# Segment sums of a four-layer graph network: gathered rows divided into three bf16 parts, one product of 390 columns a tile

## Chip, cores and metric

The kernel runs on one core of a Trainium2 chip, in one launch. The metric is the device time of a run in microseconds. Before the change three runs without a profile took 9422.37, 9434.25 and 9440.75 us; the median is 9434.25 us. The profile shown here is one further execution under the profiler.

## What is computed

6250 nodes with 128 features, and 106250 edges (`src`, `dst`) sorted by `dst`. Each of four layers is a function of `relu(layernorm(x))` that is added to `x`. What matters here are the sums over edges that each layer contains, cut to their core:

```python
support = segment_sum(xt[src], dst)                          # L0 (also the sum of edge weights a node, for L3)
out     = segment_sum(xw[src] * alpha[:, :, None], dst)      # L1, attention, alpha = softmax over a node's edges
aggA    = segment_sum(x[src] * mask_t, dst)                  # L2, for four edge types t
aggB    = segment_sum(x[dst] * mask_t, src)                  # L2, the other direction
out     = segment_sum(h[src] * norm[:, None], dst)           # L3, twice; norm = dinv[src] * w * dinv[dst]
```

`segment_sum(a, d)` adds row e of `a` to node `d[e]`. L2's weights are multiplied into the table of rows first, so that its two sums gather from a table with one row for each node and type.

## The kernel before

**Tiles and walks.** Edges lie in 832 tiles of 128, one edge a partition. A sum over the edges is a *walk*: 208 chunks of CT = 4 tiles, in a loop of 52 rounds whose body holds RING = 4 chunks (u = 0 to 3). The walks with a gather are l0, g1 (attention scores), l2, l2b (the other direction, over a list sorted by `src` that the kernel makes itself), l3a and l3b, in this order; gb, the attention sum, reads rows that were stored. Nodes lie in 49 blocks of 128. Because the edges are sorted, the 512 edges of a chunk fall into one block or into two; the second one is the `more` loop, which 48 chunks of a walk enter.

**A chunk, by engine.** Each engine has its program written by hand, and they meet at semaphores.
GpSimd (`gather`, L543; the DMA at L550) issues four indirect DMAs a chunk, each of 128 rows of 128 fp32 into GATHERED, a ring of four chunks. It waits for `free`, which says that the chunk four earlier has left its slot, and for `idx`.
ScalarE (`indices`, L834) writes the row numbers of the chunk four ahead (L831) when a chunk has landed. In l0 `weights_beside` (L859) also copies the edge weights beside the rows, as column 128.
VectorE (`aggregate` in the vector program) compares the destinations with the numbers of a block: `onehots` makes the 512-column one-hot matrix OH of the *next* chunk, in one operation (L1198) or, in l3a and l3b, in four that multiply by the edge weight as well (L1204). Then it waits for the products of this chunk and adds them to the node rows (L1220), which lie in ACC, X or T.
TensorE (`sums`, L653; the product at L658) multiplies the four one-hots with the four tiles of rows, fp32, 128 columns (129 in l0), added up in one PSUM bank; two banks take turns.
The number of further blocks, their number before this chunk and the first block come from a table, RANGES, which each engine reads into registers (L303, L306).

The order on VectorE in a chunk:

```python
onehots(c + 1, block_values((u + 1) % sets)[2], 1 - p, weights, column).then_inc(wk.onehot, 1)
hold(dve, wk.sums, c + 1)
add(first, p).then_inc(wk.added, 1)
with others(u % sets):            # the second block, where there is one
    onehots(c, b, p, weights, column).then_inc(wk.more_onehot, 1)
    hold(dve, wk.more_sums, before + w + 1)
    add(b, p).then_inc(wk.more_added, 1)
dve.nop(nofuse=True).then_inc(wk.free, 1)
```

**Work beside l0.** In l0's loop VectorE also prepares the list for l2b: in the first half, every second chunk, a comparison of 832 keys (L1356) and a count (L1365); in the second half a comparison, a scan (L1403), a product and a sum (L1406, L1408).

## Time and profile before

| | us |
|---|---|
| median of three runs without profile | 9434.25 (9422.37 to 9440.75) |
| span of the profiled execution | 11044.3 |
| time of the profiled execution outside its span | not recorded |
| GpSimd busy | 5820.6 (53%) |
| TensorE busy, products | 4003.0 (36%) |
| VectorE busy | 3958.5 (36%) |
| ScalarE busy | 1410.5 (13%) |
| TensorE clock granted, mean | 0.568 of full speed |

The profiled execution took longer than the runs. The stretches of the walks in its span, by the first and last gather: l0 from 268 to 1540 us, g1 1691 to 3223, gb some 3250 to 4280, the writes of the list 4283 to 5534, l2 to 6822, l2b 6829 to 8123, l3a 8220 to 9530, l3b 9657 to 10955. Between 4280 and 5000 the spike loop and the typed tables run.

A row of the trace gives an engine, a line of the kernel and the tiles by name (PS is PSUM, OH the one-hots, EX, H and T scratch). Idle time stands with what ended it: "issue" means that nothing visible did, "DVEq" a step of VectorE's own sequencer, "remote" a source that the trace does not know. A product of fp32 shows as two records, so a chunk's four are x8.

### The profile page before, as it was taken

What the parts mean: (1) busy time and instruction counts of PE and PEld (TensorE: products, weight loads), DVE (VectorE), ACT (ScalarE), POOL (GpSimd) and SP (SyncE); (2) the same over time, 40 slices, a digit from 0 to 9 for tenths busy, and PEclk for the clock granted to TensorE, in tenths of its full rate; (3) what the DMA queues carried; (4) which work ended last, traced back from release to release, by engine and by line L of the source; (5) the groups of instructions that cost most, each with busy time, mean ns of one, the idle gap of its engine ahead of it and who ended that gap; (6) DMA issues with size and microseconds to landing.
All of it is one profiled execution on the core that took longest, in us unless ns stands there. A gap on an engine that the chain in (4) does not pass through costs nothing. (4 is left out here: it accounts for less than half of the span.)

```text
span 11044.3 us, 116200 instructions
## 1 busy us (share of the span) xinstructions
PE 4003.0 (36%) x18072; PEld 3408.2 (31%) x18073; DVE 3958.5 (36%) x9685; ACT 1410.5 (13%) x3057; POOL 5820.6 (53%) x5941
## 2 busy tenths in 40 slices
PE   1333423333345554321033443333333333333332
PEld 1333323333335552010033333333323333233332
DVE  5335664444445557920011111111122222422224
ACT  1000011111124445710000000000000000000000
POOL 0667744555430003777766666666645565356664
PEclk6555556666665555555556665555555555555555
DMA  1111103333332221000011111111111111111111
GB/s 42 43 42 42 44 25 92 93 90 91 89 88 81 81 81 36 1 21 21 7 54 52 53 53 47 42 42 43 43 39 40 41 42 42 35 41 42 42 43 41
DMA packets 364720, 548.58 MB, mean 50 GB/s; under 512 B 124102, under 2 KB 217114, under 8 KB 364650
## 3 DMA queue, kind: packets, MB, share of 16 engines
q0 software_dynamic: 186368, 330.08, 11.1%
q1 hardware_dynamic: 148330, 190.56, 5.6%
q10 hardware_dynamic: 29952, 27.28, 1.0%
q14 instruction: 60, 0.49, 0.0%
q8 instruction: 10, 0.16, 0.0%
HBM read 448.36 MB, written 99.13 MB: 50 GB/s over the span
## 5 line engine op out<-in xcount | busy, mean ns | idle before, releaser
L658 PE MATMUL PS<-GATHERED,OH 128*128 128x128 f32 (+1 forms) x10240 | 2403.2, 416 | 4359.3 <-issue 1547.1
L658 PEld LDWEIGHTS PS<-GATHERED,OH 128*128 128x128 f32 x10240 | 2145.9, 312 | 4664.6 <-issue 2130.2
L550 POOL DMA_INDIRECT GATHERED<-row_tab,IDX x2496 | 2464.6, 987 | 1899.6 <-issue 1030.8
L550 POOL DMA_INDIRECT GATHERED<-gat_tab,IDX x832 | 784.8, 943 | 898.4 <-DVEq L1505 509.8
L575 POOL DMA_INDIRECT list_dram<-REC_NOW,PLACE_NOW x832 | 912.5, 1097 | 313.8 <-issue 258.4
L550 POOL DMA_INDIRECT GATHERED<-typed_b_tab,IDX x832 | 817.9, 983 | 483.1 <-issue 241.0
L550 POOL DMA_INDIRECT GATHERED<-typed_tab,IDX x832 | 808.9, 972 | 479.6 <-issue 234.8
L715 PE MATMUL PS<-IDENT,GATHERED 128*128 128x128 f32 x3328 | 588.1, 355 | 968.6 <-DVEq L1505 823.1
L1220 DVE TENSOR_TENSOR X<-X,PS 128x128 f32 x512 | 146.6, 286 | 2013.7 <-remote 1305.8
L715 PEld LDWEIGHTS PS<-IDENT,GATHERED 128*128 128x128 f32 x3328 | 544.3, 188 | 1012.4 <-issue 1010.5
L1204 DVE TENSOR_SCALAR OH<-IOTA,DSTF,WF 128x128 f32 x2048 | 601.1, 361 | 678.5 <-issue 648.1
L658 PE MATMUL PS<-T,OH 128*128 128x132 f32 x2048 | 541.6, 446 | 343.5 <-DVE OH L1198 292.0
L1220 DVE TENSOR_TENSOR T<-T,PS 128x128 f32 x512 | 145.7, 285 | 1237.2 <-remote 688.6
L658 PEld LDWEIGHTS PS<-T,OH 128*128 128x128 f32 x2048 | 466.0, 330 | 376.7 <-DVE OH L1198 336.4
L569 POOL COPY PLACE_NOW<-PLACE 128x16 int32 (+1 forms) x52 | 12.1, 232 | 1059.0 <-DVE ACC L1220 1059.0
L831 ACT ACTIVATE IDX<-SRCF 128x4 int32 x816 | 167.5, 205 | 2648.9 <-DMA GATHERED<-row_tab,IDX 2500.9
L1478 DVE CUSTOM_DVE_ANT_0 H<-PS,EQ 128x512 f32<-128x512 f32 x520 | 328.1, 687 | 404.8 <-remote 296.0
L1478 DVE CUSTOM_DVE_ANT_0 H<-PS,SCR 128x512 f32<-128x512 f32 x504 | 318.1, 687 | 402.9 <-remote 339.7
L1198 DVE TENSOR_TENSOR OH<-IOTA,DSTF 128x512 f32 (+1 forms) x512 | 352.5, 688 | 90.0 <-issue 86.2
L1220 DVE TENSOR_TENSOR ACC<-ACC,PS 128x129 f32 (+1 forms) x512 | 146.9, 287 | 662.9 <-PE PS L658 294.1
L754 PE MATMUL PS<-ACC,WSB 128*128 128x448 bf16 x350 | 157.8, 555 | 283.3 <-ACT ACC L975 282.0
L1198 DVE TENSOR_TENSOR OH<-IOTA,REC 128x512 f32 (+1 forms) x256 | 177.4, 693 | 172.9 <-issue 171.3
(243 smaller groups left out, 3912.5 us busy)
## 6 DMA issues: line engine op xcount, KB each, us to landing
gat_rows<-GATHERED SPq DMA_DIRECT2D x208, 264.0 KB
GATHERED<-gat_rows SPq DMA_DIRECT2D x208, 264.0 KB, 2.8
GATHERED<-row_tab,IDX POOLq DMA_INDIRECT x2496
ROWI<-dst_rows ACTq DMA_DIRECT2D x208, 128.0 KB
ROWI<-dst_rows SPq DMA_DIRECT2D x208, 128.0 KB
GATHERED<-gat_tab,IDX POOLq DMA_INDIRECT x832
list_dram<-REC_NOW,PLACE_NOW POOLq DMA_INDIRECT x832
GATHERED<-typed_tab,IDX POOLq DMA_INDIRECT x832
```

The source lines that it names most:

```text
L550: pool.indirect_dma_start(out=rows, out_offset=None, in_=table, in_offset=bass.IndirectOffsetOnAxis(ap=IDX[:, k:k + 1], axis=0),).then_inc ...
L569: pool.tensor_copy(PLACE_NOW[:, now:now + BATCH], PLACE[:, bass.ds((2 * i + k) * BATCH, BATCH)]).then_inc(batch_copied, 1)
L575: pool.indirect_dma_start(out=list_dram, out_offset=bass.IndirectOffsetOnAxis(ap=PLACE_NOW[:, now + t:now + t + 1], axis=0), in_=REC_NOW[: ...
L658: last = mm(bank(p)[:, 0:r.shape[1]], onehot(p, t), r, start=(t == 0), stop=(t == CT - 1))
L715: last = nc.tensor.transpose(bank(HEADS * (u % 2) + h)[:, t * P:(t + 1) * P], col.to_broadcast([P, P]), IDENT[:, :])
L754: last = mm(SPIKES[:, k, :], IDB, SPK[t % 2][:, k * (GB * D // 2):(k + 1) * (GB * D // 2)], start=(t == 0), stop=(t == LIF_T - 1))
L831: nc.scalar.activation(IDX[:, u * CT:(u + 1) * CT], column[:, bass.ds((RING * (i + 1) + u) * CT, CT)], ACT.Copy).then_inc(wk.idx, 1)
L1198: return v.tensor_tensor(onehot(p, 0, CT).rearrange("p (t w) -> p t w", t=CT), IOTA[:, bass.ds(b * P, P)].rearrange("p (o w) -> p o w", o= ...
L1204: last = v.tensor_scalar(onehot(p, t), IOTA[:, bass.ds(b * P, P)], DSTF[:, bass.ds(c * CT + t, 1)], weights[:, bass.ds(c * CT + t, 1)], AL ...
L1220: return v.tensor_tensor(dest, dest, bank(p)[:, 0:F], ALU.add)
L1478: last = v.tensor_tensor_reduce(out=unused[h], in0=bank(HEADS * (u % 2) + h), in1=(EQ if u % 2 == 0 else SCR)[:, :], scale=1.0, scalar=-BI ...
```

## The change

Each gathered row is divided into three bf16 parts whose sum is the row: hi = bf16(row), rest = row - hi, mid = bf16(rest), low = rest - mid. The parts stand side by side in PARTS, 130 columns apart (SEC), so that one bf16 product of 3 x 130 = 390 columns replaces the fp32 product; VectorE first adds the three sections of the bank (a reduction to COMBINED) and then adds that to the node rows. It applies to l0, l2, l2b, l3a and l3b. The attention walk gb keeps its fp32 form (`exact`).

Of a chunk, ScalarE makes hi and mid, VectorE rest (in place in GATHERED) and low. The one-hots become bf16 and are no longer weighted: in l3a and l3b VectorE multiplies the gathered rows by the edge weights instead, before the division. In l0 the weights are divided once, ahead of the walk, and ScalarE copies their three parts into column 128 of each section. PARTS holds two chunks; `parts_free` says that VectorE has finished the chunk two earlier, `free` (the ring slot) now comes with low. The table of ranges holds 16-bit numbers in rows of eight.

VectorE's order in a chunk (`chunks`):

```diff
+            if not exact:
+                if weights is not None:
+                    weigh_rows(i + (1 if u == RING - 1 else 0), c + 1, (u + 1) % RING)
+                rest(c + 1, (u + 1) % RING)
-            onehots(c + 1, block_values((u + 1) % sets)[2], 1 - p, weights, column).then_inc(wk.onehot, 1)
+            onehots(c + 1, block_values((u + 1) % sets)[2], 1 - p, column, exact).then_inc(wk.onehot, 1)
+            if not exact:
+                low(c + 1, (u + 1) % RING)
...
-            add(first, p).then_inc(wk.added, 1)
+            combine(first, p, (part_combined, c + (wk.splits * NCH + 1)), wk.added)
...
-            dve.nop(nofuse=True).then_inc(wk.free, 1)
+            dve.nop(nofuse=True).then_inc(parts_free, 1)
```

Its new functions:

```diff
+                def combine(b, p, made, added):
+                    v.tensor_reduce(COMBINED[:, 0:F], bank(p)[:, 0:NP3 * SEC].rearrange("p (k f) -> p f k", k=NP3)[:, 0:F, :],
+                                    axis=AX.X, op=ALU.add).then_inc(made[0], 1)
+                    hold(dve, *made)
+                    dest = result(b)
+                    v.tensor_tensor(dest, dest, COMBINED[:, 0:F], ALU.add).then_inc(added, 1)
+
+                def weigh_rows(i, c, u):
+                    hold(dve, wk.gathered[u], 16 * CT * (i + (wk.rounds * NIT + 1)))
+                    v.tensor_tensor(rows_of(u), rows_of(u), per_edge(weights, c, D), ALU.mult).then_inc(row_weighed, 1)
+
+                def rest(c, u):
+                    hold(dve, part_hi, c + (wk.splits * NCH + 1))
+                    v.tensor_tensor(rows_of(u), rows_of(u), parts_of(u)[:, 0, :, :], ALU.subtract).then_inc(part_rest, 1)
+
+                def low(c, u):
+                    hold(dve, part_mid, c + (wk.splits * NCH + 1))
+                    v.tensor_tensor(parts_of(u)[:, 2, :, :], rows_of(u), parts_of(u)[:, 1, :, :],
+                                    ALU.subtract).then_inc(wk.free, 1)
```

ScalarE's work for a chunk (`indices`):

```diff
+                def chunk(i, u, last_):
+                    c = RING * i + u
+                    hold(act, wk.gathered[u], 16 * CT * (i + (wk.rounds * NIT + 1)))
+                    if not last_:
+                        next_indices(wk, column, i, u)
+                    hold(act, parts_free, c + (wk.splits * NCH + 1))
+                    if weighed:
+                        hold(act, row_weighed, c + ((wk.rounds - 1) * NCH + 1))
+                    nc.scalar.activation(parts_of(u)[:, 0, :, :], rows_of(u), ACT.Copy).then_inc(part_hi, 1)
+                    if weights:
+                        nc.scalar.activation(parts_of(u, D + 1)[:, :, :, D],
+                                             WP[:, bass.ds(c * (CT * NP3), CT * NP3)].rearrange("p (t k) -> p k t", k=NP3),
+                                             ACT.Copy).then_inc(weight_kept, 1)
+                    hold(act, part_rest, c + (wk.splits * NCH + 1))
+                    nc.scalar.activation(parts_of(u)[:, 1, :, :], rows_of(u), ACT.Copy).then_inc(part_mid, 1)
```

The operand of TensorE's product, and what VectorE does ahead of l0:

```diff
+            def part_rows(u, t):
+                at = ((u % 2) * CT + t) * NP3 * SEC
+                return [PARTS[:, at:at + NP3 * SEC]]
...
+            dve.wait_ge(s_stored, 16)
+            split(WF[:, :], WREST, [WP.rearrange("p (t k) -> p k t", k=NP3)[:, k, :] for k in range(NP3)])
             dve.sem_inc(counted, 1)
+            step(v.memset(PARTS[:, :], 0.0))
+            dve.sem_inc(w_split, 1)
+            dve.sem_inc(parts_free, 2)
```

The first place is VectorE's program in the loop of l3b, from the read of the table to the add of a chunk, before (L1204 the weighted one-hots, L1220 the add; ISA rows are register steps):

```order
L303 TENSOR_LOAD RANGES
L306 ISA
L1204 TENSOR_SCALAR OH<-IOTA,DSTF,WF 128x128
L1204 ISA
L1204 TENSOR_SCALAR OH<-IOTA,DSTF,WF 128x128
L1204 ISA
L1204 TENSOR_SCALAR OH<-IOTA,DSTF,WF 128x128
L1204 ISA
L1204 TENSOR_SCALAR OH<-IOTA,DSTF,WF 128x128
L306 ISA
L54 REGISTER_ALU [waits sums_l3b]
L1220 ISA [waits added_l3b]
L1220 TENSOR_TENSOR T<-T,PS 128x128
```

and with the change, from the wait for the gather to the add (L1240 the weighing, L1244 rest, L1212 the one-hot, L1248 low, L1232 the reduction, L1236 the add):

```order
L1240 ISA [waits gathered_l0_2]
L1240 TENSOR_TENSOR GATHERED<-GATHERED,WF 128x4x128
L32 REGISTER_ALU
L1244 TENSOR_TENSOR GATHERED<-GATHERED,PARTS 128x4x128 [waits part_hi]
L298 ISA
L1212 TENSOR_TENSOR OH<-IOTA,DSTF 128x512
L1248 TENSOR_TENSOR PARTS<-GATHERED,PARTS 128x4x128 [waits part_mid]
L298 ISA
L32 REGISTER_ALU [waits sums_l0]
L1232 TENSOR_REDUCE COMBINED<-PS 128x128 [waits added_l3b]
L1236 ISA [waits part_combined]
L1236 TENSOR_TENSOR T<-T,COMBINED 128x128
```

Between the table and the wait for the products stood four one-hots and no wait; now four operations and three waits stand there, two of them for ScalarE, and the add itself has become two operations with a wait between them.

The second place is ScalarE's program in the loop of l3b, the first chunks before (L831 the row numbers):

```order
L831 ISA [waits gathered_l0_0]
L831 ACTIVATE IDX<-SRCF 128x4
L831 ISA [waits gathered_l0_1]
L831 ACTIVATE IDX<-SRCF 128x4
```

and one chunk with the change (L852 hi, L858 mid):

```order
L837 ISA [waits gathered_l0_0]
L837 ACTIVATE IDX<-SRCF 128x4
L32 ISA
L32 REGISTER_ALU [waits part_free]
L852 ACTIVATE PARTS<-GATHERED 128x4x128 [waits row_weighed]
L858 ACTIVATE PARTS<-GATHERED 128x4x128 [waits part_rest]
```

Behind the row numbers of one chunk the next chunk's wait for its gather came at once; now two copies with three waits for VectorE come between.

## Rows read from the trace of the kernel before

**Rows 1.** The page of the profiled execution: its span and part 1.

```profile
span 11044.3 us, 116200 instructions
...
PE 4003.0 (36%) x18072; PEld 3408.2 (31%) x18073; DVE 3958.5 (36%) x9685; ACT 1410.5 (13%) x3057; POOL 5820.6 (53%) x5941
```

**Rows 2.** Groups of instructions: gathers and list writes; name xcount | busy, mean ns | idle, releasers.

```profile
L550 POOL DMA_INDIRECT GATHERED<-row_tab,IDX x2496 | 2464.6, 987 | 1899.6 <-issue 1030.8 <-DVEq L1242 621.8 <-DMA row_tab<-T 224.3
...
L575 POOL DMA_INDIRECT list_dram<-REC_NOW,PLACE_NOW x832 | 912.5, 1097 | 313.8 <-issue 258.4 <-POOL REC_NOW L571 28.7 <-remote 26.7
L550 POOL DMA_INDIRECT GATHERED<-typed_b_tab,IDX x832 | 817.9, 983 | 483.1 <-issue 241.0 <-DVEq L1242 229.9 <-ACT IDX L827 6.9
L550 POOL DMA_INDIRECT GATHERED<-typed_tab,IDX x832 | 808.9, 972 | 479.6 <-issue 234.8 <-ACT IDX L831 126.6 <-DVEq L1242 118.1
L550 POOL DMA_INDIRECT GATHERED<-gat_tab,IDX x832 | 784.8, 943 | 898.4 <-DVEq L1505 509.8 <-issue 237.1 <-DMA gat_tab<-ACC 150.9
```

**Rows 3.** Timeline in l3a: start us, us, engine, line, operation [idle before <-releaser].

```profile
9012.65 1.11 DVE L1204 TENSOR_SCALAR OH<-IOTA,DSTF,WF 128x128 f32 x4 [0.67 <-issue]
...
9013.82 2.08 PE L658 MATMUL PS<-GATHERED,OH 128*128 128x128 f32 x8 [4.09 <-DVE OH L1204]
...
9020.98 0.29 DVE L1220 TENSOR_TENSOR T<-T,PS 128x128 f32 x1 [7.21 <-remote]
...
9022.03 0.94 POOL L550 DMA_INDIRECT GATHERED<-row_tab,IDX  x1 [3.96 <-DVEq L1242]
```

**Rows 4.** Gathers in l0's first half, in its second, and in l3a.

```profile
L550 POOL DMA_INDIRECT GATHERED<-row_tab,IDX x403 | 397.1, 985 | 228.2 <-issue 125.6 <-DVEq L1242 97.7 <-ACT IDX L831 2.5
...
L550 POOL DMA_INDIRECT GATHERED<-row_tab,IDX x414 | 477.0, 1152 | 150.0 <-issue 123.4 <-DVEq L1242 25.6 <-ACT IDX L831 0.9
...
L550 POOL DMA_INDIRECT GATHERED<-row_tab,IDX x824 | 780.2, 947 | 520.0 <-DVEq L1242 259.6 <-issue 250.4 <-ACT IDX L831 7.4
```

**Rows 5.** Timeline in l2b: gathers, one-hots and an add.

```profile
7301.71 0.94 POOL L550 DMA_INDIRECT GATHERED<-typed_b_tab,IDX  x1 [0.31 <-issue]
7301.77 0.69 DVE L1198 TENSOR_TENSOR OH<-IOTA,REC 128x512 f32 x1
...
7302.52 2.08 PE L658 MATMUL PS<-GATHERED,OH 128*128 128x128 f32 x8 [8.71 <-DVE OH L1198]
...
7304.79 0.29 DVE L1220 TENSOR_TENSOR X<-X,PS 128x128 f32 x1 [2.33 <-issue]
7305.78 0.69 DVE L1198 TENSOR_TENSOR OH<-IOTA,REC 128x512 f32 x1 [0.70 <-issue]
7305.83 1.46 POOL L550 DMA_INDIRECT GATHERED<-typed_b_tab,IDX  x1 [0.68 <-issue]
```

**Rows 6.** Groups of instructions, shapes apart: prices of VectorE's and ScalarE's operations.

```profile
L1198 DVE TENSOR_TENSOR OH<-IOTA,DSTF 128x512 f32 x504 | 347.0, 688 | 86.5 <-issue 83.3 <-DVE H L1365 1.5
...
L831 ACT ACTIVATE IDX<-SRCF 128x4 int32 x816 | 167.5, 205 | 2648.9 <-DMA GATHERED<-row_tab,IDX 2500.9 <-issue 138.5 <-DMA GATHERED<-gat_tab,IDX 5.7
...
L1220 DVE TENSOR_TENSOR X<-X,PS 128x128 f32 x512 | 146.6, 286 | 2013.7 <-remote 1305.8 <-PE PS L658 607.1 <-issue 98.2
...
L1403 DVE TENSOR_TENSOR_SCAN EX<-ONE,H,EX 128x832 f32<-128x832 f32 x50 | 97.5, 1951 | 9.8 <-issue 5.7 <-DVE EX L1356 4.1
...
L1356 DVE TENSOR_SCALAR EX<-EX,KCOL 128x832 f32<-128x832 f32 x102 | 73.0, 716 | 32.6 <-issue 32.6
L1534 DVE TENSOR_REDUCE AT_EDGE<-PS 128x32 f32<-128x96 f32 x256 | 65.9, 258 | 206.1 <-PE PS L723 90.3 <-issue 87.4 <-DVE AT_EDGE L1534 28.4
...
L1365 DVE TENSOR_REDUCE H<-EX 128x832 f32 x52 | 53.0, 1020 | 11.8 <-DVE EX L1356 6.8 <-issue 5.0
...
L811 ACT ACTIVATE GATHERED<-H 128x896 f32 x24 | 22.6, 941 | 0.0
```

**Rows 7.** Busy time and clock in l3a; then the bf16 product of the spike counts.

```profile
8225.00:9525.00 1300.00, 489.35 (x2016) 434.00 (x2016) 363.69 (x1257) 41.87 (x204) 780.17 (x824) 0.53 0.14 42
...
L754 PE MATMUL PS<-ACC,WSB 128*128 128x448 bf16 x350 | 157.8, 555 | 283.3 <-ACT ACC L975 282.0 <-issue 1.2
```

More of the change, by code:

```diff
@@ L31 @@
 I16 = mybir.dt.int16
+U16 = mybir.dt.uint16
 BF16 = mybir.dt.bfloat16
@@ L545, in gather @@
                 hold(pool, wk.free, c + 1)
-                hold(pool, wk.idx, c + 1)
+                hold(pool, wk.idx, c + (wk.splits * NCH + 1))
                 for t in tiles:
@@ L656, in sums @@
                 for t in range(CT):
-                    r = rows(t)
-                    last = mm(bank(p)[:, 0:r.shape[1]], onehot(p, t), r, start=(t == 0), stop=(t == CT - 1))
+                    for n, r in enumerate(rows(t)):
+                        last = mm(bank(p)[:, 0:r.shape[1]], onehot(p, t, 1, r.dtype == F32), r, start=(t == 0 and n == 0),
+                                  stop=(t == CT - 1 and n == len(rows(t)) - 1))
                 return last
@@ L671, in chunk @@
                     hold(pe, wk.added, c + 1)
-                    sums(lambda t: rows(u, t), wk.onehot, c, u % 2).then_inc(wk.sums, 1)
+                    sums(lambda t: rows(u, t), wk.onehot, c + wk.splits * NCH, u % 2).then_inc(wk.sums, 1)
                     with others(u % sets):
@@ L845, in indices @@
                     start += n
+                for u in range(RING):
+                    chunk(NIT - 1, u, True)
             for req in requests["before_l0"]:
@@ L851, in _ @@
                 answer(*req)
-            wk = walks["l0"]
-            first_indices(wk, SRCF)
-            def weights_beside(i, last_):
-                for u in range(RING):
-                    c = RING * i + u
-                    hold(act, wk.gathered[u], 16 * CT * (i + 1))
-                    nc.scalar.activation(G3[:, u * CT:(u + 1) * CT, D], WF[:, bass.ds(c * CT, CT)],
-                                         ACT.Copy).then_inc(weight_kept, 1)
-                    if not last_:
-                        next_indices(wk, SRCF, i, u)
-            with act.Fori(0, NIT - 1) as i:
-                weights_beside(i, False)
-            weights_beside(NIT - 1, True)
+            act.wait_ge(w_split, 1)
+            indices("l0", weights=True)
             for req in requests["l0_sums"]:
@@ L1024, in _ @@
             dense(dn, denses["l3a"], 4)
-            indices("l3a")
+            indices("l3a", weighed=True)
             for req in requests["l3a"]:
@@ L1028, in _ @@
             dense(dn, denses["l3b"], 5)
-            indices("l3b")
+            indices("l3b", weighed=True)
             for req in requests["l3b"]:
@@ L1216, in aggregate @@
                 wk = walks[name]
+                exact = ahead is not None
                 def add(b, p):
@@ L1249, in aggregate @@
                     read(0, 0, table)
-                onehots(0, block_values(0)[2], 0, weights, column).then_inc(wk.onehot, 1)
+                if not exact:
+                    if weights is not None:
+                        weigh_rows(0, 0, 0)
+                    rest(0, 0)
+                onehots(0, block_values(0)[2], 0, column, exact).then_inc(wk.onehot, 1)
+                if not exact:
+                    low(0, 0)
                 start = 0
```

110 lines of the change are left out of this document (66 added, 44 removed).

## The prediction

> **What bounds the kernel now.** I read the page first. GpSimd is the busiest engine, 5820.6 us of a span of 11044.3 us; TensorE, which the change relieves, is busy for 36% of it [rows 1]. Nearly all of GpSimd's time is row gathers, 832 in each of six walks over the edges, and 832 writes of a list [rows 2]. A walk has 208 chunks of 4 gathers.
>
> Next the timeline of an l3a stretch. While nothing is late, gathers take 0.94 us with 0.30 us between (as in [rows 5]), 1.25 us each and 5.0 us a chunk; TensorE's four products of a chunk take 2.08 us. Then the pattern breaks: TensorE is done at 9015.90, VectorE adds those sums only at 9020.98, released by nothing that the trace knows, and GpSimd waits 3.96 us for the ring slot that VectorE frees behind the add [rows 3]. I take these stalls for the recording's own: the median run without a profile is 9434.25 us, 1610 us shorter than the recorded span (the record gives no other time for that execution). GpSimd's idle time before gathers and list writes sums to 4074.5 us; less 5824 x 0.305 us of usual gap (1776) and two waits for a table's store (224.3 + 150.9, [rows 2]), 1923 us are left. If all that the median saves is of these waits, 313 us of them remain in it, 0.25 us a chunk.
>
> The changed walks are therefore bound by **GpSimd's issue**: 4 x (mean gather + 0.305) is 5.11 us a chunk in l2 and 5.15 in l2b [rows 2], 5.16 in l0's first half, 5.83 in its second and 5.01 in l3a and l3b [rows 4]. I work out differences in these numbers and add them to the median; added to the recorded span they would carry the recorder's stalls along.
>
> **Why gathers differ in length.** A gather that starts 0.05 us behind the start of a one-hot, which has two SBUF inputs, takes 1.46 us instead of 0.94; a one-hot that starts 0.06 us behind a gather keeps its 0.69 us, and the gather its 0.94 [rows 5]. l0's second half, where scans of 1.95 us run on VectorE [rows 6], has a mean of 1.152 us [rows 4]. So a two-input VectorE operation on SBUF delays a gather that starts while it runs. One-hots run 256 times a walk, 208 for first blocks and 48 for second ones (512 adds for two walks [rows 6]), 1.23 a chunk. In l2b they cost 4 x (0.983 - 0.944) = 0.16 us a chunk, 0.13 us for each.
>
> **The change, per chunk.**
> Removed: the four fp32 products (2.08 us) become four bf16 ones of 390 columns. By columns that is 4 x 390 against four passes of 4 x 128, so 2.08 x 1560/2048 = 1.6 us at the same clock (0.53 granted, close to the 1.2 GHz level [rows 7]). Bounds: 2.2 us by the bf16 product of 448 columns, 0.555 us each [rows 7], and 0.8 at twice the clock. For first blocks this lies under VectorE's next chunk and is worth nothing; only a second block waits for it.
> Added on ScalarE: two copies of 512 elements. 896 take 0.941 us and 4 take 0.205, so by the line between them 0.62 [rows 6]; ends 0.55 and 0.72.
> Added on VectorE: rest and low, 512 elements and two inputs each, 0.69 us as the one-hot [rows 6]. In l3a and l3b also the weighing, 0.69, while four one-hots of together 1.11 [rows 3] become one of 0.69. The add of 0.29 becomes a reduction of 384 PSUM elements and an add of 0.29. The reduction lies between 96 elements at 0.258 and 832 at 1.020, by that line 0.56 [rows 6]; ends 0.45 and 0.75, should the stride between the three sections help or hurt.
> Moved: a ring slot is freed behind low instead of behind the add. That helps GpSimd only where slots were short, the 0.25 us above at most. The 16-bit range table is read in as many loads as before; I cost it at nothing, as it lies between VectorE's commands in the start below.
>
> Now the order on VectorE. While it splits chunk c+1 it waits twice for ScalarE, whose first copy may begin only when VectorE has finished chunk c-1, and in l3 only behind the weighing. All that is queued behind these waits, the add of chunk c among it, stands still. For a change of engine I allow 0.15 us, between one-hot to product, 0.06 [rows 3], and product to add, 0.19 (7302.52 + 2.08 to 7304.79 [rows 5]), with ends 0.06 and 0.30; within VectorE 0.10.
> l3: start 0.70 (0.67 seen [rows 3]) + weigh 0.69 + (0.15 + copy 0.62 + 0.15) + rest 0.69 + (0.15 + second copy 0.62 + 0.15, over the one-hot's 0.69) + low 0.69 + reduce 0.56 + 0.10 + add 0.29 = 5.56. Second blocks, 48 in 208: 0.69 + 1.6 + 0.24 + 0.56 + 0.10 + 0.29 = 3.48, or 0.80 a chunk. Together **6.4 us**, over GpSimd's 5.0, so the chain of VectorE and ScalarE sets the pace.
> l2, l2b: no weighing, and the first copy (0.92 and 0.10 of waits) runs beside the start: 1.02 + 0.69 + 0.92 + 0.69 + 0.95 + 0.80 = 5.1. GpSimd meets two more two-input operations and the short add: 5.13 + 2.2 x 0.13 = **5.42**, the larger of the two.
> l0: 5.1 plus the bucket work beside, (0.72 + 1.02)/2 + 0.1 = 1.0 in the first half and (0.72 + 1.95 + 1.02 + 1.02)/2 + 0.1 = 2.5 in the second (its product and sum taken as the count of as many elements, 1.02 [rows 6]), less 0.2 for the copy that runs beside it: **5.9** and **7.4**.
>
> Sum: l3a and l3b 416 x (6.4 - 5.01) = 578; l2 and l2b 416 x (5.42 - 5.13) = 121; l0 104 x (5.9 - 5.16) + 104 x (7.4 - 5.83) = 240; splitting the weights and clearing the parts ahead of l0, five operations of 1 to 2 us, 10. That is +949, and 9434 + 949 = **10380 us**.
> Ends: with handovers of 0.06, a reduction of 0.45 and a start of 0.5, l3 takes 5.65 and l0 5.3 and 6.8: 266 + 121 + 15 + 101 + 10 = +513, less the waits that the median may still have in walks that VectorE now paces (0.25 x 624 = 156), +357. With handovers of 0.30, copies of 0.72, a reduction of 0.75 and second blocks 0.4 longer: l3 7.5, l2 6.1, l0 7.0 and 8.5, +1920. Each end needs all at once; half of the way to them is 10090 and 10870, this case's own range.
>
> A rule weighed here. One-hots take 0.69 us in the mean of 504 [rows 6], though gathers fill three quarters of the time and one is seen to start inside a gather without loss [rows 5]. The Trainium skill (SBUF — State Buffer, "Who interferes with whom") says that a VectorE instruction with two SBUF inputs contends with a GpSimd instruction that reads SBUF, and that whichever starts second fully blocks until the first has ended. The late gather agrees with it; the other direction, VectorE held by a running gather, no row here shows.
>
> **Rivals.**
> A. *GpSimd still paces every walk* (0.14). VectorE's commands overlap more than I allow and l3 stays near 5.5 us. Against it: each step of the chain waits for one on another engine. Then l3 costs 416 x (5.55 - 5.01) = 225, l2 121, l0 130, and 10 ahead: 9920.
> B. *Blocked both ways* (0.03). A two-input operation that starts inside a gather waits for its rest. Gathers fill 0.944 of 1.25 us, so each waits 0.76 x 0.47 = 0.36 us: 1.5 us for 4.2 operations in l3, 1.2 for 3.2 elsewhere, of which l2's slack takes 0.3. That is 416 x 1.5 + 416 x 0.9 + 208 x 1.2 = 1250 more, 11630. The one-hots at 0.69 speak against. It is also what the page's rule gives if it holds in both directions.
> C. *Handovers dearer* (0.09). Registers and waits cost 0.3 us each, six to eight a chunk: l3 7.2, l2 5.9, l0 6.7 and 8.2, so 911 + 320 + 407 + 10: 11080.
> D. *Faster* (0.04). The 313 us that the median can hold are real waits for ring slots in VectorE's order. Freed behind low, not behind products and add, the five changed walks lose them: 0.25 x 1040 = 260, 9170. It decides only where VectorE's chain stays under 5.0 us a chunk; l0's second half, with 2.5 us of bucket work on top, speaks against it, and so does every sum above.
> E. *No difference* (0.03). The chain fits under the gathers, and the ring waits saved pay for the longer gathers: 9434.
>
> **How the numbers follow.** The likeliest case has 0.67 and gives the time. The range 9870 to 11000 holds nearly all of it, A's middle and the cheaper part of C; B, D, E and the rest, about 0.2, are out. A measurement can tell about 0.2% (19 us) from no change: faster 0.04 (D), within it 0.03 (E), slower 0.93.
>
> **What would show it.** In the changed profile, away from the recorder's stalls: gathers of l3a and l3b that wait for VectorE's low; an l3 chunk of 6.4 us; l0's second half the slowest stretch; l2's gathers at a mean near 1.05 us; copies at 0.62, the reduction at 0.56 and a chunk's four products at 1.6 us; VectorE busy some 2000 us more, TensorE less. The prediction is wrong if VectorE stands idle in l3 while gathers follow each other at 1.25 us, or if rest, the one-hot or low take much less than 0.69 us.

## The result and the profile after

| | before | changed |
|---|---|---|
| median of four runs each, us | 9435.38 | 10835.39 |
| lowest to highest, us | 9422.37 to 9440.75 | 10834.68 to 10839.15 |
| ratio, with its interval | | 1.1486 (1.147 to 1.1502) |
| span of the profiled execution, us | 11044.3 | 10834.0 |

The change makes the kernel slower by 1400 us. The forecast was 10380 us in a range of 9870 to 11000: the direction and the range hold, but a loss of 946 us was forecast, some 450 less than came.

The page of the changed kernel: span, part 1, two rows of part 4 (the chain that ended last), and the groups that answer to [rows 2] and [rows 6].

```profile
span 10834.0 us, 121338 instructions
...
PE 3498.6 (32%) x12952; PEld 1802.1 (17%) x12953; DVE 6027.9 (56%) x11930; ACT 2636.4 (24%) x5137; POOL 6072.7 (56%) x5941
...
DVE 29%; issue 23%; DVEq 14%; POOL 13%; ACT 9%; PE 8%; DMA 2%; ACTq 0%; SPq 0%; POOLq 0%
DVEq L295 9%; POOL list_dram L576 8%; DVE COMBINED L1232 6%; DVE GATHERED L1244 6%; PE PS L659 6%; ACT PARTS L858 5%; POOL GATHERED L551 4%; ACT PARTS L852 3%; DVE GATHERED L1240 3%; DVE OH L1212 2%; DVE H L1533 2%; DVEq L34 2%; DVE PARTS L1248 1%; PE PS L721 1%; DMA GATHERED<-gat_tab,IDX 1%
...
L551 POOL DMA_INDIRECT GATHERED<-row_tab,IDX x2496 | 2562.0, 1026 | 2187.8 <-DVE PARTS L1248 1053.6
L659 PE MATMUL PS<-PARTS,OH 128*128 128x390 bf16 x5120 | 1880.5, 522 | 5451.6 <-issue 1578.3
L1244 DVE TENSOR_TENSOR GATHERED<-GATHERED,PARTS 128x512 f32<-128x512 f32 x1040 | 720.2, 693 | 1849.9 <-ACT PARTS L852 1703.1
...
L551 POOL DMA_INDIRECT GATHERED<-typed_tab,IDX x832 | 896.6, 1078 | 274.3 <-issue 233.7
L551 POOL DMA_INDIRECT GATHERED<-typed_b_tab,IDX x832 | 885.0, 1064 | 271.5 <-issue 228.6
...
L1232 DVE TENSOR_REDUCE COMBINED<-PS 128x128 f32<-128x384 f32 (+1 forms) x1280 | 708.7, 554 | 421.4 <-PE PS L659 417.2
```

Read them in this order. TensorE has 500 us less to do and VectorE 2070 us more [rows 1]. The row gathers, which in [rows 2] waited for VectorE only where its steps came late, now wait 1053.6 us for low (L1248), the operation that frees a ring slot; in l2 and l2b nearly all of their idle time is the usual 0.3 us gap, but each gather is longer (1.078 and 1.064 us, 0.972 and 0.983 before). Rest (L1244) waited 1703.1 us for ScalarE's first copy. In the chain that ended last VectorE's own queue (DVEq, its register and semaphore instructions) stands with 14%, of which the page puts 9% on L295; that line is the load of the range table.

A chunk of l3a in the timeline of the changed kernel (start us, us, engine, line, operation, [idle before <-releaser]; TensorE's weight loads left out):

```profile
8732.48 0.29 DVE L1236 TENSOR_TENSOR T<-T,COMBINED 128x128 f32 x1 [0.20 <-DVE COMBINED L1232]
...
8733.51 1.48 PE L659 MATMUL PS<-PARTS,OH 128*128 128x390 bf16 x4 [4.61 <-DVE T L1236]
...
8734.05 0.69 DVE L1240 TENSOR_TENSOR GATHERED<-GATHERED,WF 128x512 f32<-128x512 f32 x1 [1.28 <-issue]
8734.83 0.63 ACT L852 ACTIVATE PARTS<-GATHERED 128x512 bf16<-128x512 f32 x1 [3.84 <-DVE GATHERED L1240]
...
8735.57 0.69 DVE L1244 TENSOR_TENSOR GATHERED<-GATHERED,PARTS 128x512 f32<-128x512 f32 x1 [0.83 <-ACT PARTS L852]
8736.18 0.69 DVE L1212 TENSOR_TENSOR OH<-IOTA,DSTF 128x512 bf16 x1
8736.35 0.63 ACT L858 ACTIVATE PARTS<-GATHERED 128x512 bf16<-128x512 f32 x1 [0.89 <-DVE GATHERED L1244]
8736.43 1.25 POOL L551 DMA_INDIRECT GATHERED<-row_tab,IDX  x1 [0.30 <-issue]
...
8737.08 0.69 DVE L1248 TENSOR_TENSOR PARTS<-GATHERED,PARTS 128x512 bf16<-128x512 f32 x1 [0.22 <-ACT PARTS L858]
8737.69 0.55 DVE L1232 TENSOR_REDUCE COMBINED<-PS 128x128 f32<-128x384 f32 x1
8738.44 0.29 DVE L1236 TENSOR_TENSOR T<-T,COMBINED 128x128 f32 x1 [0.20 <-DVE COMBINED L1232]
8738.65 0.94 POOL L551 DMA_INDIRECT GATHERED<-row_tab,IDX  x1 [0.97 <-DVE PARTS L1248]
...
8740.09 0.69 DVE L1240 TENSOR_TENSOR GATHERED<-GATHERED,WF 128x512 f32<-128x512 f32 x1 [1.36 <-issue]
```

From one weighing to the next it is 6.04 us, and every step of the forecast's chain can be read: weigh, 0.09, copy 0.63, 0.11, rest, one-hot, 0.09 behind rest the second copy, 0.10, low, reduction, 0.20, add. TensorE's 1.48 us lie beside it. Then comes the long one: 1.28 and 1.36 us from the add to the next weighing, in which VectorE issues only register and semaphore work.

### The profile page after: what moved, and what is told of

It reads as the page before. It is cut to its first block, busy times and chain, and to the rows that moved or that the text cites. A ratio compares the mean times of both kernels' runs of the same rounds, so it can differ in the third digit from the quotient of the medians.

```text
span 10834.0 us, 121338 instructions
## 1 busy us (share of the span) xinstructions
PE 3498.6 (32%) x12952; PEld 1802.1 (17%) x12953; DVE 6027.9 (56%) x11930; ACT 2636.4 (24%) x5137; POOL 6072.7 (56%) x5941
## 4 chain that ended last, share of the span: by engine, by line
DVE 29%; issue 23%; DVEq 14%; POOL 13%; ACT 9%; PE 8%; DMA 2%; ACTq 0%; SPq 0%; POOLq 0%
DVEq L295 9%; POOL list_dram L576 8%; DVE COMBINED L1232 6%; DVE GATHERED L1244 6%; PE PS L659 6%; ACT PARTS L858 5%; POOL GATHERED L551 4%; ACT PARTS L852 3%; DVE GATHERED L1240 3%; DVE OH L1212 2%; DVE H L1533 2%; DVEq L34 2%; DVE PARTS L1248 1%; PE PS L721 1%; DMA GATHERED<-gat_tab,IDX 1%
## 5 line engine op out<-in xcount | busy, mean ns | idle before, releaser
L551 POOL DMA_INDIRECT GATHERED<-row_tab,IDX x2496 | 2562.0, 1026 | 2187.8 <-DVE PARTS L1248 1053.6
L659 PE MATMUL PS<-PARTS,OH 128*128 128x390 bf16 x5120 | 1880.5, 522 | 5451.6 <-issue 1578.3
L1244 DVE TENSOR_TENSOR GATHERED<-GATHERED,PARTS 128x512 f32<-128x512 f32 x1040 | 720.2, 693 | 1849.9 <-ACT PARTS L852 1703.1
L659 PEld LDWEIGHTS PS<-PARTS,OH 128*128 128x128 bf16 x5120 | 555.4, 130 | 6802.0 <-issue 5639.0
L852 ACT ACTIVATE PARTS<-GATHERED 128x512 bf16<-128x512 f32 x1040 | 656.0, 631 | 2872.8 <-DVE GATHERED L1240 1916.4
L551 POOL DMA_INDIRECT GATHERED<-typed_tab,IDX x832 | 896.6, 1078 | 274.3 <-issue 233.7
L858 ACT ACTIVATE PARTS<-GATHERED 128x512 bf16<-128x512 f32 x1040 | 655.2, 630 | 1499.3 <-DVE GATHERED L1244 1499.3
L1232 DVE TENSOR_REDUCE COMBINED<-PS 128x128 f32<-128x384 f32 (+1 forms) x1280 | 708.7, 554 | 421.4 <-PE PS L659 417.2
L1248 DVE TENSOR_TENSOR PARTS<-GATHERED,PARTS 128x512 bf16<-128x512 f32 x1040 | 720.0, 692 | 237.8 <-ACT PARTS L858 236.4
L1212 DVE TENSOR_TENSOR OH<-IOTA,DSTF 128x512 bf16 (+3 forms) x1024 | 703.3, 687 | 7.5
L1240 DVE TENSOR_TENSOR GATHERED<-GATHERED,WF 128x512 f32<-128x512 f32 x416 | 288.4, 693 | 631.8 <-issue 587.1
```

The lines of the kernel that those rows point to most:

```text
L551: pool.indirect_dma_start(out=rows, out_offset=None, in_=table, in_offset=bass.IndirectOffsetOnAxis(ap=IDX[:, k:k + 1], axis=0),).then_inc ...
L659: last = mm(bank(p)[:, 0:r.shape[1]], onehot(p, t, 1, r.dtype == F32), r, start=(t == 0 and n == 0), stop=(t == CT - 1 and n == len(rows(t ...
L852: nc.scalar.activation(parts_of(u)[:, 0, :, :], rows_of(u), ACT.Copy).then_inc(part_hi, 1)
L858: nc.scalar.activation(parts_of(u)[:, 1, :, :], rows_of(u), ACT.Copy).then_inc(part_mid, 1)
L1212: return v.tensor_tensor(onehot(p, 0, CT, exact).rearrange("p (t w) -> p t w", t=CT), IOTA[:, bass.ds(b * P, P)].rearrange("p (o w) -> p o ...
L1232: v.tensor_reduce(COMBINED[:, 0:F], bank(p)[:, 0:NP3 * SEC].rearrange("p (k f) -> p f k", k=NP3)[:, 0:F, :], axis=AX.X, op=ALU.add).then_i ...
```

## The experiments

Twelve runs in three lots; three of them repeat a kernel. The kernel before is run beside each lot, and gave 9434 us beside the first, 11005 beside the second and 10903 beside the third, each on another chip. So times are compared within a lot only. Each chip stood in one lot, so what belongs to the chip and what to other circumstances of a lot can't be told apart; "chip" below means both. In the code cuts `...` marks lines left out.

### First lot: which part of the change costs what

**e1_before_u16**: the kernel before with the range tables of the change (16 bits, 8 elements a chunk, of which 4 are read), and nothing else.

```diff
-        RANGES = sb("RANGES", [1, REGS * NCH], I32)
+        RANGES = sb("RANGES", [1, ROW * NCH], U16)
...
-                eng.load(regs[p], table[0:1, bass.ds(c * REGS, REGS)])
+                eng.load(regs[p], table[0:1, bass.ds(c * ROW, REGS)])
```

> The kernel before with nothing changed but the table of ranges: 16-bit numbers in rows of eight, as the change has it. Theory 1 (a read of the 16-bit table takes 0.95 us instead of 0.34 and that is a part of the change's loss): the gathered walks stay as they are, since GpSimd's 5.0 us a chunk covers VectorE's 2.5 to 3.1; gb, which has no gather and reads the table on three engines, loses about 1 us a chunk: 9640 us. Theory 2 (the reads are hidden; the prediction's chain of VectorE and ScalarE is merely longer): 9435 us.

Measured: 9547.53 us, ratio 1.0121 (1.0104 to 1.0138), so the table costs the old kernel 114 us. The trace's records of the loads to registers say why: on VectorE one takes 0.948 us in the median of 1464 (0.344 us for the 32-bit table in the profile of before), on ScalarE 0.887 (0.308), on TensorE 0.987 (0.332). The cost is smaller than the 9640 us expected, because the edge walk gb, the only one in which a load was expected to show, loses some 0.55 us a chunk and not 1: from the last gather of g1 to the first write of the list it takes 1085 us in e2 with the 32-bit table and 1199 in the changed kernel.

This profile has a second use. Its span is 9548.9 us, as long as its runs without a profile, and it has none of the stalls of [rows 3]. So it is the clean picture of the old order of work, but for the wider loads. The gathers of its l3b:

```profile
L551 POOL DMA_INDIRECT GATHERED<-row_tab,IDX x832 | 789.0, 948 | 380.3 <-issue 246.2 <-DMA row_tab<-T 127.1 <-DVEq L1243 7.0
```

They wait 7.0 us in all for the slot that VectorE frees behind products and add; in the other walks that the change touches it is 6.7 (l3a), 12.5 (l2), 15.2 (l2b) and 5.5 and 27.3 us (l0's halves). That is 74 us, and, apart from the ends of walks, about the most that any cheaper product could have given back while the gathers stay as they are.

The windows of e1, for l0 (two halves), g1, the edge walk gb, l2, l2b, l3a and l3b (columns: window, its length, busy time and count of PE, PEld, DVE, ACT and POOL, granted clock, DMA share, GB/s):

```profile
267.00:802.00 535.00, 258.32 (x1008) 224.62 (x1008) 211.02 (x354) 33.08 (x206) 408.53 (x416) 0.52 0.19 51
802.00:1412.00 610.00, 261.57 (x1020) 228.04 (x1020) 373.11 (x496) 33.05 (x205) 476.66 (x416) 0.51 0.17 45
1567.00:2607.00 1040.00, 588.26 (x3312) 530.74 (x3312) 685.65 (x2285) 221.04 (x458) 784.77 (x832) 0.75 0.52 134
2608.00:3801.00 1193.00, 605.11 (x3088) 516.03 (x3088) 575.57 (x1883) 415.94 (x722) 0.34 (x2) 0.50 0.26 70
5029.00:6083.00 1054.00, 562.68 (x2186) 448.91 (x2187) 246.58 (x508) 96.15 (x351) 800.74 (x832) 0.59 0.23 65
6092.00:7151.00 1059.00, 511.69 (x2040) 445.88 (x2040) 246.99 (x511) 41.91 (x204) 805.27 (x832) 0.54 0.20 51
7246.00:8290.00 1044.00, 514.16 (x2040) 451.86 (x2040) 355.77 (x1278) 41.87 (x204) 790.64 (x832) 0.51 0.20 52
8417.00:9459.00 1042.00, 514.19 (x2040) 450.79 (x2040) 355.06 (x1278) 41.87 (x204) 788.75 (x832) 0.52 0.20 52
```

And the same stages of the changed kernel:

```profile
274.00:880.00 606.00, 179.89 (x492) 53.82 (x492) 399.97 (x671) 152.81 (x405) 428.67 (x416) 0.50 0.17 45
880.00:1671.00 791.00, 188.28 (x516) 56.95 (x516) 575.34 (x824) 155.81 (x414) 448.67 (x416) 0.50 0.13 35
1847.00:2887.00 1040.00, 589.35 (x3312) 532.58 (x3312) 685.04 (x2286) 219.32 (x458) 784.94 (x832) 0.75 0.52 134
2888.00:4086.00 1198.00, 605.43 (x3088) 516.11 (x3088) 575.58 (x1881) 415.39 (x721) 0.34 (x2) 0.50 0.26 70
5313.00:6483.00 1170.00, 462.22 (x1155) 149.65 (x1155) 638.65 (x1167) 325.41 (x762) 895.96 (x832) 0.54 0.21 58
6502.00:7640.00 1138.00, 374.27 (x1013) 109.70 (x1014) 644.76 (x1174) 296.89 (x618) 884.67 (x832) 0.50 0.18 48
7738.00:9159.00 1421.00, 371.26 (x1004) 108.76 (x1004) 775.53 (x1366) 280.54 (x614) 837.05 (x832) 0.50 0.15 38
9305.00:10726.00 1421.00, 371.28 (x1004) 108.75 (x1004) 775.63 (x1367) 278.51 (x614) 845.74 (x832) 0.50 0.15 38
```

Divided by 208 chunks (104 for a half), before stood at 5.15 and 5.87 us in l0, 5.07 in l2, 5.09 in l2b and 5.01 in l3a and l3b; the changed kernel at 5.83 and 7.61, 5.63, 5.47 and 6.83. The stages differ by 252 us in l0, 195 in l2 and l2b together and 756 in l3a and l3b. With the 114 us of the table in the edge walk (the windows of 1193 and 1198 us both hold it) these make 1317 of the 1400 us; the rest lies outside these stretches, at starts and ends of walks, and was not taken apart.

**e2_after_i32**: the changed kernel with the 32-bit table of before; the loaded values go through a register of their own and a maximum with zero.

```diff
...
-                eng.load(regs[p], table[0:1, bass.ds(c * ROW, REGS)])
+                eng.load(raw[p], table[0:1, bass.ds(c * REGS, REGS)])
+                for loaded_, r in zip(raw[p], regs[p]):
+                    eng.reg_alu(r, loaded_, 0, ALU.max)
```

> The changed kernel with the table in 32-bit numbers as before, loaded into registers of their own and held at 0 or more by one register step each. Theory 1: l3a and l3b lose 0.6 us a chunk (6.83 to 6.2, 250 us together), l0 0.3 (60), l2 and l2b little (30), gb about 1 us (200): 10300 us. Theory 2: 10835 us, the chunk times unchanged.

Measured: 10397.72 us (10391.57 to 10401.34), ratio 1.1022 (1.1004 to 1.1041): 438 us below the changed kernel, where some 535 were expected. The width of a table of 208 rows is nearly a third of the whole loss. The timeline of e2 shows the step, and l3b's window the pace:

```profile
8822.33 0.29 DVE L1239 TENSOR_TENSOR T<-T,COMBINED 128x128 f32 x1 [0.20 <-DVE COMBINED L1235]
...
8823.38 0.69 DVE L1243 TENSOR_TENSOR GATHERED<-GATHERED,WF 128x512 f32<-128x512 f32 x1 [0.76 <-issue]
```

```profile
8978.00:10294.00 1316.00, 371.33 (x1004) 108.85 (x1004) 777.14 (x1369) 278.54 (x614) 909.10 (x832) 0.50 0.16 41
```

The start is 0.76 us where it was 1.28 to 1.36, and a chunk 1316/208 = 6.33 us instead of 6.83. In the trace's records the load takes 0.947 us of that start of 1.36 and 0.343 of the 0.76; the rest is 0.41 and 0.42, so the maximum with zero costs next to nothing here. Of the 438 us, 2 x 105 lie in l3a and l3b; in l0 the two halves go to 5.47 and 7.19 us, 80 us; the edge walk gives back 113.

**e3_after_i32_three**: e2 with the three parts multiplied one behind the other into the same 130 columns of the bank, 12 products a chunk instead of 4, so that TensorE adds the three sums and VectorE's reduction goes.

```diff
-                return [PARTS[:, at:at + NP3 * SEC]]
+                return [PARTS[:, at + k * SEC:at + (k + 1) * SEC] for k in range(NP3)]
...
-                    v.tensor_reduce(COMBINED[:, 0:F], bank(p)[:, 0:NP3 * SEC].rearrange("p (k f) -> p f k", k=NP3)[:, 0:F, :], axis=AX.X, op=ALU.add).then_inc(made[0], 1)
-                    hold(dve, *made)
-                    v.tensor_tensor(dest, dest, COMBINED[:, 0:F], ALU.add).then_inc(added, 1)
+                    add(b, p).then_inc(added, 1)
```

> As e2, and each tile's one product of 390 columns becomes three of 130 that add up in the same 130 columns of the bank; VectorE adds them to the node rows directly, without the reduction. If the chain on VectorE sets the pace, the reduction and the wait behind it (0.56 + 0.10, 1.23 times a chunk) come off l3a, l3b and l0: 0.8 x 624 = 500 us less than e2, about 9800; l2 and l2b stay at GpSimd's 5.4 us. If TensorE's products are on the path, 12 weight loads a chunk instead of 4 cost more than they give: the same as e2 or slower.

Measured: 9959.78 us, ratio 1.0558 (1.0541 to 1.0576), again 438 us less, where 500 were expected: 296 in l3a and l3b, 98 in l0, nothing in l2 and l2b. In its timeline TensorE's twelve products of 130 columns take 1.48 us together, as the four did: the 390 columns were no gain over three times 130.

**e4_after_i32_noweigh**: e2 without the weighing in l3a and l3b; the edge weights are left out of these two walks.

```diff
-            indices("l3a", weighed=True)
+            indices("l3a")
...
-                aggregate(name, lambda b: T[:, bass.ds(b * D, D)], D, WF)
+                aggregate(name, lambda b: T[:, bass.ds(b * D, D)], D)
```

> As e2, with the weighing of the gathered rows left out of l3a and l3b (their edge weights are left out of the computation). If the serial order weighing, first copy, rest sets l3's pace, a chunk falls from 6.2 to l2's 5.45, where GpSimd takes over: 320 us less than e2, about 9980. If GpSimd sets l3's pace already in e2, no more than 50 us less.

Measured: 10073.01 us, ratio 1.0681 (1.0663 to 1.0699), 325 us below e2, close to the 320 expected. The gathers of l3b, in e2:

```profile
L554 POOL DMA_INDIRECT GATHERED<-row_tab,IDX x832 | 909.1, 1093 | 546.0 <-issue 383.4 <-DVE PARTS L1251 162.6
```

in e3:

```profile
L554 POOL DMA_INDIRECT GATHERED<-row_tab,IDX x832 | 916.4, 1101 | 382.2 <-issue 354.8 <-DVE PARTS L1247 26.2 <-ACT IDX L840 1.2
```

and in e4:

```profile
L554 POOL DMA_INDIRECT GATHERED<-row_tab,IDX x832 | 910.2, 1094 | 382.4 <-issue 364.4 <-DVE PARTS L1251 17.7 <-ACT IDX L840 0.3
```

What follows: taking 0.75 us (reduction and handover) or 0.69 us (weighing) out of VectorE's chain takes 0.71 and 0.74 us off an l3 chunk, 6.33 to 5.62 and 5.59, so the chain was the bound. Both stop at the same place, with the wait for low (PARTS) down from 163 us to 26 and 18. There GpSimd paces again, at 4 x (1.10 + 0.30) = 5.6 us and no longer at 5.0: each gather is 0.15 us longer than in e1. Both versions stand on that floor, and a version of the split that avoids it was not measured on this chip.

Why the gathers are longer, e2's trace shows one by one. In l3b 515 of the 832 gathers start while a two-input operation of VectorE runs, and take 1.18 us in the mean, with 0.6 us of the operation left 1.38 and with 0.3 left 1.10; the other 317 take 0.943. In the changed kernel, at its slower pace, only 227 start so, and the mean is 1.02. So an operation has no fixed price: e4 has one two-input operation a chunk fewer than e3, and its gathers are as long. The other way round nothing is lost: of e2's 867 two-input operations in that walk the 412 that start inside a gather take 0.689 us and the others 0.693.

### Second lot: the old order, on a chip with stalls

All four start from the kernel before with the clamped reads of e2.

**f1_before_clamp** is that base.

> The kernel before with the range table left at 32 bits, loaded to registers of its own and held at zero or above by four register operations per read; the same computation. It is the base of the next three runs. In the gather walks the reads lie under the four gathers of a chunk (5.01 us), in the edge walk gb they are on the chain. Theory (only the width of the load costs): 9440 to 9480 us. Rival (the reads cost by their count of register operations): as the 16-bit table, 9550 us.

Measured: 11035.55 us, ratio 1.0023 (1.0004 to 1.0043) to the kernel before, which itself took 11004.69 us here. The clamped reads cost 0.2% in the old order, where little waits for them. The expectation's absolute times fail with the chip. Its profile (span 11035.0 us) looks like the profile of before (11044.3), the gathers of l3b too:

```profile
L553 POOL DMA_INDIRECT GATHERED<-row_tab,IDX x832 | 789.1, 948 | 619.3 <-issue 272.0 <-DVEq L1245 200.8 <-DMA row_tab<-T 126.5
```

Gathers of 0.948 us as ever, but the freed slot (L1245) comes late. In the trace some register and semaphore instructions of VectorE, ScalarE, TensorE and SyncE take 0.7 or 1.4 us, in bursts, where e1, table loads and branches aside, has none over 0.21 us; GpSimd's stay under 0.1 us in both.

**f2_before_scalar** makes the one-hots of l0, l2 and l2b by four compares with one input each.

```diff
...
+                    for t in range(CT):
+                        last = v.tensor_scalar(onehot(p, t), IOTA[:, bass.ds(b * P, P)], column[:, bass.ds(c * CT + t, 1)],
+                                               None, ALU.is_equal)
+                    return last
```

> The base with the one-hots of l0, l2 and l2b made by four tensor_scalar compares of 128x128 (about 1.1 us together) and no longer by one two-input operation of 128x512 (0.69 us); the same computation. Theory (a gather that begins under a two-input VectorE operation is held up by some 0.13 us, and nothing else of VectorE is on the chain): mean gather of l2 and l2b from 0.97 to 0.95 us, chunk from 5.08 to 5.02 us, l0 5.15 to 5.03 in its first half; 45 to 60 us below the base. Rival (VectorE's length counts): 0.43 us more per one-hot on second blocks, 30 to 100 us above the base.

Measured: 11046.75 us, ratio 1.0042 (1.0023 to 1.006). The mean gather of l2 and l2b falls from 0.975 (f1) to 0.946 us, as the theory has it; the time does not fall, as here a chunk takes 6.1 to 6.2 us by the stalls, and shorter gathers are paid for with longer waits. Inconclusive for a chip without stalls.

**f3_before_extra** adds work that nobody waits for: in l3a two subtractions a chunk with two inputs, in l3b two multiplications with one.

```diff
+                            if name == "l3a":
+                                for k in range(2):
+                                    v.tensor_tensor(DUM[:, (2 * p + k) * CE:(2 * p + k + 1) * CE], EQ[:, :], H[:, 0:CE], ALU.subtract)
+                            if name == "l3b":
+                                for k in range(2):
+                                    v.tensor_scalar(DUM[:, (2 * p + k) * CE:(2 * p + k + 1) * CE], EQ[:, :], 1.0, None, ALU.mult)
```

> The base with VectorE work added that nobody waits for: in each chunk of l3a two subtractions of two 128x512 tiles (0.69 us each, two sources in SBUF), in each chunk of l3b two multiplications of one 128x512 tile by a number (one source). Theory: the two-input ones hold up gathers by 0.13 us each, l3a from 5.01 to 5.28 us a chunk, +55 us; the one-source ones hold up nothing, l3b stays at 5.01. Rival 1 (VectorE has room, 2.5 of 5 us): both walks unchanged. Rival 2 (any VectorE work beside a gather counts): both walks slower alike.

Measured: 11050.99 us, ratio 1.0034 (1.001 to 1.0057), 15 us over f1 and not told from it. The walks' pace did not move under the stalls. The gathers did: 1.108 us in l3a and 1.02 in l3b, where f1 has 0.947.

**f4_before_half** multiplies two of a chunk's four tiles only, and so leaves out half of each sum in the five walks.

```diff
-                for t in range(CT):
+                n = CT if rows(0).shape[1] == XW else CT // 2
+                for t in range(n):
```

> The base with only two of a chunk's four tiles multiplied in l0, l2, l2b, l3a and l3b: it leaves out half of each sum there. Theory (TensorE's products are under the gathers, so that bf16 products could save nothing): chunks of l2, l2b, l3a and l3b unchanged at 5.0 to 5.1 us, only the second half of l0 (two and more blocks a chunk, 5.87 us) gains, 0 to 40 us below the base. Rival (products are on the chain): 1.0 us of 2.08 less for each of 1040 chunks, 1000 us below.

Measured: 10952.37 us, ratio 0.9953 (0.9936 to 0.997): 83 us below f1, and not 1000. Half of TensorE's products gone is worth 0.75% on this chip, and the change takes less off them (2.08 to 1.48 us a chunk). It is more than the 0 to 40 us of the theory, but of the size of the 74 us that e1's waits allow. No cheaper product could have made this kernel much faster.

### Third lot: on another chip with stalls

**g1_scalar_again** is f2 again.

> The kernel before with clamped 32-bit reads and scalar one-hots in l0, l2 and l2b, once more, since in the last batch the kernel before itself took 11005 us on its chip (9434 in the first) and stalls of 0.7 us in loops lay over a chunk's pace there. If this chip gives 9434 for the kernel before: theory 9390 to 9430 us (gathers of l2 and l2b 0.945 us, chunk 5.00); rival (length of VectorE's work counts) 9470 to 9550. If it gives 11005: 11040 again, as before within 0.5%.

Measured: 11038.02 us beside 10902.79, ratio 1.0107 (1.0072 to 1.0141): the second of the two cases named. The kernel beside it has no clamped reads, and f1 was not run again, so the loss of 1.1% can't be put down to the compares; a gain there is not.

**g2_extra_again** is f3 again.

> The base with two extra two-input subtractions a chunk in l3a and two extra one-input multiplications a chunk in l3b, once more for the same reason. The last batch had mean gathers of 1.10 us in l3a and 1.02 in l3b where the base had 0.947, with the chunk's pace unchanged at 6.2 us under the stalls. Where the kernel before takes 9434: l3a 4 x 0.15 more, 5.6 us a chunk, l3b 4 x 0.07, 5.3 us a chunk, together +90 to +100 us over 9434 to 9480. Rival (gathers' mean grows but the pace does not, since their start waits for something else): both walks 5.0, no change.

Measured: 10969.29 us, ratio 1.0068 (1.0046 to 1.009), again with the clamped reads in it. Its gathers and extra operations, in l3a:

```profile
L554 POOL DMA_INDIRECT GATHERED<-row_tab,IDX x832 | 919.1, 1105 | 456.0 <-issue 241.1 <-DVEq L1252 107.4 <-DMA row_tab<-T 98.6
...
L1238 DVE TENSOR_TENSOR DUM<-EQ,H 128x512 f32<-128x512 f32 x412 | 264.7, 683 | 0.0
```

and in l3b:

```profile
L554 POOL DMA_INDIRECT GATHERED<-row_tab,IDX x831 | 845.2, 1017 | 540.1 <-issue 256.1 <-DVEq L1252 143.7 <-DMA row_tab<-T 124.8
...
L1241 DVE TENSOR_SCALAR DUM<-EQ 128x512 f32<-128x512 f32 x410 | 156.0, 422 | 0.0
```

The gathers' lengths repeat those of f3 to 0.01 us. Against f1's 0.948 two two-input operations a chunk lengthen four gathers by 4 x (1.105 - 0.948) = 0.63 us, 0.31 for each; two one-input ones by 0.28, 0.14 for each. Meanwhile the two-input operations keep their 0.68 us, though gathers fill most of the time: GpSimd waits for VectorE, and VectorE not for GpSimd. That a longer gather becomes a longer chunk where GpSimd paces is not shown by this run, whose pace is the stalls'; it is what e3 and e4 show. The Trainium skill (SBUF — State Buffer, "Who interferes with whom") has both kinds in its rule, the two-input operation and the one-input operation in a two-port mode; that the multiplication ran in such a mode is suggested by its 0.42 us alone, against 0.68 for the subtraction of as many elements. The longer gathers agree with it. By that rule VectorE would be held as well when it starts second; the measurement differs, and decides: in l3a here the 338 two-input operations that start inside a gather take 0.683 us, the 74 others 0.684.

**g3_after_again** is the changed kernel, unaltered.

> The changed kernel as it is. Where the kernel before takes 9434 us: 10835 again, ratio 1.149. Where it takes 11005: theory (the stalls lie on VectorE's and TensorE's loops; GpSimd's gathers hid part of them before, and nothing hides them now) 12400 to 12900, ratio 1.13 to 1.17; rival (the stalls are waiting time that both share) 11300 to 12000, ratio 1.03 to 1.09.

Measured: 11782.72 us beside 10902.79, ratio 1.08 (1.0782 to 1.0818). This is the rival's case; the theory failed. The windows of l3a and l3b are 1434 us each:

```profile
8665.00:10099.00 1434.00, 371.24 (x1004) 109.01 (x1004) 776.25 (x1368) 280.49 (x614) 836.55 (x832) 0.50 0.15 38
10242.00:11676.00 1434.00, 371.25 (x1004) 108.99 (x1004) 776.11 (x1367) 278.21 (x614) 843.25 (x832) 0.50 0.15 38
```

That is 13 us more than on the chip without stalls, where the old order loses some 250 (l3a took 1292 us in f1, on the second chip, and 1044 in e1). So the same change costs 15% on one chip and 8% on another: the old order takes 1469 us more here than on the chip without stalls, the new one 947. Of those 947, 457 lie in g1, which the change does not touch (1497 us and 1040).

**g4_after_i32_three_nolow** is e3 without the subtraction that makes the low parts; they stay zero, and the sums lose them.

```diff
-                    v.tensor_tensor(parts_of(u)[:, 2, :, :], rows_of(u), parts_of(u)[:, 1, :, :],
-                                    ALU.subtract).then_inc(wk.free, 1)
+                    dve.nop(nofuse=True).then_inc(wk.free, 1)
```

> The change with the 32-bit table and three products (9960 us) without the subtraction that makes the low parts: they stay zero, so the sums lose the low part of every row. VectorE has 0.69 us less a chunk, everything else is issued as before. Theory (what is left of the loss is gathers held up by VectorE's two-input operations): mean gather of l3 from 1.10 to 1.05, its chunk from 5.60 to 5.4, l2 from 5.5 to 5.35, together 9790 to 9880 us. Rival (the row buffers come free too late, after low): the chunk falls to 5.0 to 5.1 in every walk, 9500 to 9600. Rival 2 (another wait paces it): 9960.

Measured: 11871.07 us, ratio 1.0888 (1.0869 to 1.0906), above the unchanged new kernel in the same lot, though it does less than e3, which took 9960 on the first chip. All three expectations, made from 9960 us, fail. Its l3 gathers take 1.008 us, but that does not speak for the theory: in g3, which makes low, they take 1.006 and 1.014 at about the same slow pace. GpSimd waits for the freed slot again:

```profile
L554 POOL DMA_INDIRECT GATHERED<-row_tab,IDX x553 | 557.3, 1008 | 444.4 <-DVEq L1247 278.4 <-issue 163.9 <-ACT IDX L840 2.1
```

(1000 us of l3b), and its timeline has holes of 6 us and more in VectorE's work that g3's l3 walks do not have. Which loops the stalls strike, and why this one and not g3's, stays open. No kernel of the study that computes the full sums is faster than the kernel before.

## Why the prediction was right, and where it was off

**The bound.** Right: GpSimd's issue paced the old walks. Without stalls (e1) l0 is at 5.15 and 5.87 us, l2 and l2b at 5.07 and 5.09, l3 at 5.01; the forecast read 5.16, 5.83, 5.11, 5.15 and 5.01 out of a profile that was 17% too long, by taking a gather's mean and the usual gap and leaving the waits out. The 74 us that e1's gathers wait for freed slots, and f4, show the other half of it: TensorE was not in the way.

**The stalls.** Wrong as to their cause. They are not the recorder's own: e1 to e4 and the changed kernel have profiled spans within 2 us of their unprofiled times, and on two other chips the kernel before takes 10.9 to 11.0 ms without a profile. They come with the chip, or with what else its lot had. To reckon in differences and add them to the median was still the right use, since the times were from a chip without them. The 0.25 us a chunk that the median might have kept is hardly there (5.01 us is four bare gathers; e1's 74 us are 0.07 a chunk), and with it falls the ground of rival D.

**The step that failed: "I cost it at nothing".** The 16-bit table has as many loads, but each takes 0.95 instead of 0.34 us on VectorE, and the place named as its cover, between VectorE's commands in the start, is on the chain itself. The start was put at 0.70 us and is 1.28 to 1.36; with the 32-bit table it is 0.76. e2 puts the price at 438 us in all. With that table the kernel takes 10398 us where 10380 was forecast.

**The other terms**, in us:

| | forecast | measured |
|---|---|---|
| copy on ScalarE | 0.62 | 0.63 |
| reduction | 0.56 | 0.55 |
| four products | 1.6, at 0.53 granted | 1.48, at 0.50 |
| from one engine to another | 0.15 | 0.09 to 0.11 |
| reduction to add | 0.10 | 0.20 |
| second blocks, a chunk | 0.80 | 6.83 - 6.04 = 0.79 |
| VectorE's busy time, more | 2000 | 2070 |

An l3 chunk is 6.83 us against 6.4 forecast, 6.33 in e2. l0 came at 5.83 and 7.61 (5.9 and 7.4), in e2 at 5.47 and 7.19, so its forecast was 0.2 to 0.4 too dear and the table hid that. l2 and l2b came at 5.63 and 5.47 against 5.42; e2, with 5.5 and 5.6, shows that this term was mis-sized without the table too. The price of a two-input operation to the gathers was read from one operation a chunk as 0.13 us. Two more in l2 made it 4 x (1.078 - 0.963) = 0.46, 0.23 each, and in g2 two back to back made 0.31 each: what counts is how many gathers start under one, which the forecast took as fixed.

That 10398 and 10380 agree so well is therefore part luck: by e2's windows against e1's, l3 and l0 were 32 and 68 us too high, l2 and l2b 71 too low, and 44 us at the ends of walks were not counted.

**Rivals.** A (GpSimd still paces every walk) holds for l2 and l2b, and for l3 only once the reduction or the weighing is gone (e3, e4). B (blocked both ways) is out: two-input operations kept 0.69 us. C came nearer in size (11080) by the wrong term: handovers are cheaper than allowed, and 0.6 us sits in one load. D and E are out.

## What to carry to other kernels

Before an engine is relieved, look whether anybody waits for it: here half of TensorE's products were worth 0.75%, while the new VectorE operations lengthened the chain where it paces and, where it doesn't, the gathers that start under them. A sum over parts can be left to TensorE, in the same bank columns: here twelve products of 130 columns took as long as four of 390, and saved the reduction. Cost every load of a register when its element type changes, as any other instruction, above all where an engine has nothing else to do at that place.
